# Attention and experts of eight images: the pairs of maxima in later images placed by another table

## The chip, the cores and the metric

The kernel runs on one core of a Trainium2 chip. The metric is the device time of one execution in microseconds, as the median of timed runs. The engines are TensorE (PE, its weight loads PEld), VectorE (DVE), ScalarE (ACT), GpSimd (POOL) and SyncE (SP), which here issues DMAs.

## The reference

One transformer layer with modulation (adaLN) over 8 images of 1024 tokens by 256 channels, in float32:

```python
mod = (silu(c) @ wmod)                 # sa, ca, ga, sb, cb, gb per image
h = layernorm(x) * (1 + ca) + sa
kv_c = rmsnorm(h @ W_kv) * g_kv;  q_c = h @ W_q
q, k = concat(content, rope(...))      # 16 heads of 16 + 32 channels
attn = softmax(causal(q @ k.T * scale))
x = x + ga * ((attn @ v) @ W_o)
h = layernorm(x) * (1 + cb) + sb
t = (h @ Wm + bm) in tokens x 8 heads of 32
w = softmax(t @ expert_emb); top 2 of 16 experts
out = sum over the 2: w * (gelu(t @ W1[e] + b1) @ W2[e] + b2)
x = x + gb * (out @ Wo + bo)
```

## The kernel before, in words

Each engine has its own program, and all five walk the same lists. An image has two parts. The attention part is 48 slots (`MAIN`): a slot is one group g of four heads, one half c of the queries (512 tokens) and one block j of 128 keys. `SEQ` orders the group-halves: slots 0 to 3 are (0,0), 4 to 7 (1,0), 8 to 15 (0,1), 16 to 19 (2,0), 20 to 23 (3,0), 24 to 31 (1,1), 32 to 39 (2,1), 40 to 47 (3,1). The last four blocks of each are diagonal and have 512, 384, 256 and 128 columns, the others 512. In a slot TensorE computes the scores in two steps of two heads (`scores(s, 0)`, `scores(s, 1)`, L1279), ScalarE takes the exponentials (L1393), and in even slots TensorE multiplies with the values of the two slots before (`values`, L1305). Four PSUM banks hold scores, two steps deep. The experts' part is 64 steps, with L1321, L1411, L1339, L1448 and L1518.

Softmax needs the maximum of each query's row before the scores are made. It enters as one more row of the queries, against minus ones in the keys. The maxima are computed apart, in "pairs": a pair is a tile of queries by keys for two heads (hh = 0, 1), two matmuls into two banks of a ring (L428), and two reads by VectorE, which take the maximum (L576; L573 where the causal mask is added, some of them in two pieces). Group g has five pairs for the first half (`PAIRS[0]`) and thirteen for the second (`PAIRS[1]`). When a group-half is done, an item `("row", g, c)` transposes the maxima (L500), VectorE copies them (L586), and SyncE sends them with four DMAs (L780) into the queries, on which the first scores of that group-half wait (semaphore `c_row..`). For the second half an `rmax` item (L582) joins two columns first.

`attend_slots(img)` writes the list of items by hand: each slot has three parts, "between" (after `scores(s, 0)`), "behind" (after `scores(s, 1)`) and "front" (after that), then come the values. Other items are `rope` (rotary parts, L477 or L479, L607, L608, and L726, L739 on GpSimd), `sums` (outputs divided, L505, L595, L598), `tr` (L510), `o` (output projection, L518, L634), `stats`, `xn`, `tr2`, `tm`, and `chain` (the router). All of them share one ring of three PSUM banks, in the order of the list; a pair takes two. `ring_write` waits for both banks before the pair's first matmul. An item's bank is free when its reader (VectorE, or ScalarE for some) has incremented `c_rd` or `c_ra`.

For images 1 to 7 `PLACES` gives each of the 47 pairs a slot and a part. Two pairs of group 1 were made in the experts' part of the image before (`AHEAD`). Image 0 has a list of its own, which the change leaves alone. In it, slot 12 holds three pairs (`(12, 3)` with part `2 * k // n`: two between, one behind), slot 22 holds one, and slot 25 holds two and a `sums` item.

VectorE also multiplies the gates into two projection weights and a bias, five instructions after the items of slot 22: `wog` (attention's projection), `wfg` (the last projection) and `bog`. TensorE waits for them once, before `("o", 0, 0)` in slot 32, and GpSimd before it adds `bog` at the start of the experts' part.

Of the kernel before, what the change touches and what calls it, by code (L numbers as in the profile page):

```python
# [23 lines left out]
CH = C // P  # L24
# [312 lines left out]
PAIRS = [masked_pairs(0), [(((i, 0, pr),),) for i in range(4, 8) for pr in range(2)]]  # L337
# [74 lines left out]
def item_matmuls(pe, L, R, item):  # L412
# [57 lines left out]
    elif kind == "rope":  # L470
        g, isk, c = rope_of(item[1], R.alone)
        if g < 2:
            R.wait(pe, L, ("ht", c, CH - 1) if isk else ("qct", c))
        hd = slice(g * HG * RD, (g + 1) * HG * RD)
        if isk:
            for k in range(CH):
                mm = pe.matmul(out, L.wkr[:, k, hd], L.ht[:, k, half(c)], start=(k == 0), stop=(k == CH - 1))  # L477
        else:
            mm = pe.matmul(out, L.wqr[:, hd], L.qct[:, half(c)], start=True, stop=True)  # L479
    elif kind == "sum":  # L480
        R.wait(pe, L, ("kvt",))
        for t in range(4):
            mm = pe.matmul(out[:, 2 * t:2 * t + 2], L.kvsq[:, t * P:(t + 1) * P], L.halves[:, :], start=True, stop=True)
    elif kind == "qc":
        h, c = item[1:]
        R.wait(pe, L, ("qct", c))
        mm = pe.matmul(out, L.wqc[:, h * P:(h + 1) * P], L.qct[:, half(c)], start=True, stop=True)  # L487
    elif kind == "std":
        pe.wait_ge(S["f_ks"], 1)
        for t in range(4):  # L490
            for c in range(2):
                mm = pe.matmul(out[KVR * c:KVR * c + KVR, t * P:(t + 1) * P],
                               L.kstd[:, 4 * c + t:4 * c + t + 1].broadcast_to([P, KVR]), L.ident[:, :], start=True, stop=True)
    elif kind == "row":
        g, c = item[1:]
        if c:
            pe.wait_ge(S["c_mf"] if g else S["f_mf"], max(g, 1))
        else:
            R.wait(pe, L, ("pair", g, *PAIRS[0][-1]))
        mm = pe.transpose(out[0:4 * HG, 0:P], L.mxf if c else L.mx0[:, g, :], L.ident[:, :])  # L500
    elif kind == "sums":
        m = item[1]
        pe.wait_ge(S["c_o"], m + 1)
        for t in range(4):
            mm = pe.transpose(out[:, t * P:(t + 1) * P], L.ot[:, m % 2, t * P:(t + 1) * P], L.ident[:, :])  # L505
    elif kind == "tr":
        c, j = item[1:]
        R.wait(pe, L, ("sums", SEQ.index((NG - 1, c))))
        for t in range(4):
            mm = pe.transpose(out[:, t * P:(t + 1) * P], L.ao[:, 4 * c + t, j * P:(j + 1) * P], L.ident[:, :])  # L510
    elif kind == "o":
        c, n = item[1:]
        R.wait(pe, L, ("tr", c, CH - 1))
        if c == 0:
            pe.wait_ge(S["d0_w"], 5)
        for t in range(2):
            for k in range(CH):
                mm = pe.matmul(out[:, t * C:(t + 1) * C], L.at[:, k, (2 * n + t) * P:(2 * n + t + 1) * P], L.wog[:, k, :],  # L518
                               start=(k == 0), stop=(k == CH - 1))
    elif kind == "tr2":  # L520
        c, j = item[1:]
        pe.wait_ge(S[f"d{c}_xn"], 4)
        for t in range(4):
            mm = pe.transpose(out[:, t * P:(t + 1) * P], L.xn2[:, t, j * P:(j + 1) * P], L.ident[:, :])
    elif kind == "tm":
        c, j = item[1:]
        R.wait(pe, L, ("tr2", c, CH - 1))
        for k in range(CH):
            mm = pe.matmul(out, L.wms[:, k, j * P:(j + 1) * P], L.h2t[:, k, :], start=(k == 0), stop=(k == CH - 1))  # L529
    elif kind == "lg":  # L530
        c = item[1]
        R.wait(pe, L, ("tm", c, CH - 1))
        for t in range(4):
            for j in range(CH):
                o = t * P + j * 4 * NE
                mm = pe.matmul(out[:, o:o + 4 * NE], L.t32[:, j, t * P:(t + 1) * P], L.embd[:, :], start=True, stop=True)  # L536
    elif kind == "gt":
        c = item[1]
        pe.wait_ge(S[f"d{c}_r"], 17)
        for t in range(4):  # L540
            mm = pe.transpose(out[:, t * P:(t + 1) * P], L.eb[:, t * FH:(t + 1) * FH, :].rearrange("p a b -> p (a b)"),
                              L.ident[:, :])
    elif kind == "out":
        n = item[1]
        pe.wait_ge(S["e_add"], 30 * (n // 2 + 1))
        for t in range(2):
            for k in range(CH):
                mm = pe.matmul(out[:, t * C:(t + 1) * C], L.ct[:, k, (2 * n + t) * P:(2 * n + t + 1) * P], L.wfg[:, k, :],  # L548
                               start=(k == 0), stop=(k == CH - 1))
# [553 lines left out]

AHEAD = 2
EARLY = 3
PLACES = [(1, 0), (2, 0), (3, 0), (5, 0), (7, 0)]
PLACES += [(s, part) for s in range(9, 37) for part in range(2 - s % 2)]


def attend_slots(img):  # L1110


    slots = [([], [], []) for _ in range(NM)]
    if img:
        slots[1][1].extend([("out", 2), ("out", 3)])
        places = PLACES
        pairs = [("pair", 1, *p) for p in PAIRS[1][AHEAD:AHEAD + 5]]
        pairs += [("pair", g, *p) for g in (2, 3) for p in PAIRS[0]]
        pairs += [("pair", 1, *p) for p in PAIRS[1][AHEAD + 5:]]
        pairs += [("pair", g, *p) for g in (2, 3) for p in PAIRS[1]]  # L1120
    else:
        per_slot = [(0, 2), (1, 2), (2, 3), (3, 2), (4, 3), (5, 3), (8, 2), (9, 1), (10, 2), (11, 2), (12, 3), (13, 1), (14, 2), (15, 1),
                    (16, 2), (17, 2), (18, 2), (19, 1), (20, 2)] + [(s, 1 if s in (22, 23, 27, 29, 31, 33) else 2) for s in range(21, 37)]
        places = [(s, 2 * k // n) for s, n in per_slot for k in range(n)]
        early, second = [("pair", 0, *p) for p in PAIRS[1][EARLY:]], [("pair", 1, *p) for p in PAIRS[1]]
        pairs = early[:1] + [("pair", 1, *p) for p in PAIRS[0]] + early[1:]
        pairs += second[:5] + [("pair", 2, *p) for p in PAIRS[0]] + second[5:6] + [("pair", 3, *p) for p in PAIRS[0]] + second[6:]
        pairs += [("pair", g, *p) for g in (2, 3) for p in PAIRS[1]]
        slots[2][1].append(("row", 1, 0))
        slots[6][0].append(("rmax", 0))  # L1130
        slots[6][1].append(("row", 0, 1))
    assert len(places) == len(pairs)
    ropes = {s: ("rope", 8 + k) for k, s in enumerate((0, 2, 3, 4, 5, 6, 7, 8) if img else (3, 5, 6, 7, 8, 9, 10, 11))}
    for (s, part), pair in zip(places, pairs):
        if part and img and s and s in ropes:
            slots[s][1].append(ropes.pop(s))
        slots[s][part].append(pair)
    for s, rope in ropes.items():
        slots[s][1].append(rope)
    for s, g in ((21, 1), (29, 2), (37, 3)):  # L1140
        slots[s][0].insert(0, ("rmax", g))
    for s, row in ((13, (2, 0)), (17, (3, 0)), (21, (1, 1)), (29, (2, 1)), (37, (3, 1))):
        slots[s][2].append(("row", *row))
    for m, gc in enumerate(SEQ[:-1]):
        last = max(s for s, step in enumerate(MAIN) if step[:2] == gc)
        slots[last + 2][2].append(("sums", m))
    slots[27][1].append(("tr", 0, 0))
    slots[28][1].append(("tr", 0, 1))
    slots[32][1].append(("o", 0, 0))
    slots[33][1].extend([("o", 0, 1), ("stats", 0)])  # L1150
    slots[34][1].append(("xn", 0))
    slots[37][1].extend([("tr2", 0, 0), ("tr2", 0, 1)])
    slots[38][1].append(("tm", 0, 0))
    slots[39][1].extend([("tm", 0, 1), ("tlo", 0, 0)])
    slots[40][1].extend([("tlo", 0, 1), ("lg", 0), ("chain", 0, 1), ("chain", 0, 2)])
    slots[41][1].append(("exp", 0))
    for k in range(3, 18):
        slots[41 + (k - 3) // 3][1].append(("chain", 0, k))
    slots[46][2].append(("gt", 0))
    return slots  # L1160
# [68 lines left out]
def all_images(nc, L, O):  # L1229
# [18 lines left out]
    with nc.Block() as block:  # L1248
# [182 lines left out]
        def _(v):  # L1431
# [29 lines left out]
            for img in range(B):  # L1461
                for s, (between, behind, front) in enumerate(aslots[img]):
# [6 lines left out]
                    if s == 22:  # L1469
# [3 lines left out]
                        for k in range(CH):  # L1473
                            v.tensor_tensor(L.wog[:, k, :], L.wos[:, k, :], L.gate[:, 0, :],
                                            ALU.mult).then_inc(S["d0_w"], 1)
                            v.tensor_tensor(L.wfg[:, k, :], L.wfs[:, k, :], L.gate[:, 1, :],
                                            ALU.mult).then_inc(S["d0_w"], 1)
                        v.tensor_tensor(L.bog[:, :], L.bor[:, :], L.gate[:, 1, :], ALU.mult).then_inc(S["d0_w"], 1)
# [214 lines left out]
```

## Time and profile before

| | us |
|---|---|
| median of 3 timed runs | 2917.65 (2917.25 to 2918.07) |
| the profiled execution | 2920.5 |
| its span, first to last instruction | 2918.1 |
| attention part of the third image (window) | 161.00 |

The span is what the trace shows; the profiled execution's own time has 2.4 us more around it. Busy time is an engine's union of instructions; a matmul's end is modelled, so a step of TensorE is best read as the distance between starts.

### The profile page before, as it was taken

The numbers are of one execution on the slowest core, as the hardware profiler recorded it, in microseconds if no ns is written. First come the engines' busy times: TensorE is split into PE (matmuls) and PEld (weight loads), VectorE is DVE, ScalarE is ACT, GpSimd is POOL, SyncE is SP. The second block draws the span as 40 slices with busy tenths as digits, with TensorE's granted clock in tenths as the row PEclk, the third lists the DMA queues.
The fourth block names the chain that finished last, engine by engine and source line by source line (L and its number), as shares of the span: only waits on it lengthen the run. The fifth ranks groups of instructions, "written<-read, shape, count | busy, mean of one in ns | idle before, by whom it ended". The sixth has DMA issues, their size and how long they took to land.

```text
span 2918.1 us, 50109 instructions
## 1 busy us (share of the span) xinstructions
PE 2816.6 (97%) x16476; PEld 1241.9 (43%) x16476; DVE 1863.0 (64%) x4638; ACT 1808.5 (62%) x2148; POOL 1246.2 (43%) x1325
## 2 busy tenths in 40 slices
PE   7899999999999999999999999999999999999999
PEld 3344444444444443444444444444444444444433
DVE  5775666756666666666667666675756657667553
ACT  2346675566755677457675576655666566665687
POOL 4312645136451364414654146531565215561254
PEclk9899999999999999999999999999999999999999
DMA  6203453044430444304432055311453124530343
GB/s 156 57 5 99 118 130 73 1 108 122 120 71 8 119 118 107 71 21 121 122 97 61 23 134 130 87 47 46 121 133 89 32 71 119 124 88 20 77 127 94
DMA packets 176972, 252.96 MB, mean 87 GB/s; under 512 B 50509, under 2 KB 83293, under 8 KB 176621
## 3 DMA queue, kind: packets, MB, share of 16 engines
q1 hardware_dynamic: 176100, 248.44, 34.3%
q8 instruction: 136, 2.23, 0.3%
q10 hardware_dynamic: 620, 1.34, 0.2%
q14 instruction: 116, 0.95, 0.1%
HBM read 159.13 MB, written 12.63 MB: 59 GB/s over the span
## 4 chain that ended last, share of the span: by engine, by line
PE 86%; DVE 7%; issue 3%; ACT 2%; POOL 1%; SPq 1%; DMA 1%; ACTq 0%; DVEq 0%; POOLq 0%
PE ps L1279 17%; PE ps L1321 17%; PE ps L1339 16%; PE ps L1305 9%; PE ps L428 7%; PE ps L477 4%; PE ps L479 2%; PE ps L518 2%; PE ps L548 2%; DVE rest L573 1%; PE ps L529 1%; PE ps L505 1%; PE ps L536 1%; PE ps L463 1%; PE ps L487 1%
## 5 line engine op out<-in xcount | busy, mean ns | idle before, releaser
L1411 ACT ACTIVATE rest<-ps 128x1024 f32<-128x1024 f32 x1024 | 993.8, 1024 | 341.1 <-PE ps L1321 340.9
L1393 ACT ACTIVATE rest<-ps 128x1024 f32<-128x1024 f32 (+3 forms) x768 | 610.2, 809 | 537.4 <-PE ps L1279 511.6
L1518 POOL TENSOR_TENSOR rest<-rest 128x512 f32<-128x512 f32 x478 | 632.0, 1322 | 560.7 <-DVE rest L1448 548.1
L1448 DVE SCALAR_TENSOR_TENSOR rest<-ps,b2c,wide 128x512 f32<-128x512 f32 x512 | 384.0, 750 | 489.8 <-PE ps L1339 451.7
L1321 PE MATMUL ps<-wide,w1s 98*128 98x512 f32 x2048 | 655.1, 437 | 11.5 <-ACT rest L1411 8.7
L1339 PE MATMUL ps<-rest,w2s 128*32 128x512 f32 x4096 | 546.1, 605 | 0.6 <-ACT rest L1411 0.6
L1508 POOL TENSOR_SCALAR_AFFINE_SELECT rest<-rest 128x256 f32<-128x256 f32 x512 | 206.4, 411 | 772.3 <-ACT rest L1393 770.3
L573 DVE CUSTOM_DVE_ANT_0 rest<-ps,maskd 128x512 f32<-128x512 f32 (+3 forms) x1024 | 444.8, 487 | 118.8 <-PE ps L428 114.0
L1279 PE MATMUL ps<-wide 49*128 49x512 f32 (+3 forms) x2304 | 486.3, 511 | 10.2 <-ACT rest L1393 4.2
L1321 PEld LDWEIGHTS ps<-wide,w1s 98*128 98x128 f32 x2048 | 340.8, 188 | 301.0 <-ACT rest L1411 189.0
L576 DVE TENSOR_REDUCE front<-ps 128x1 f32<-128x512 f32 x512 | 329.0, 684 | 92.9 <-PE ps L428 88.7
L428 PE MATMUL ps<-wide 48*128 48x512 f32 (+3 forms) x1152 | 269.9, 500 | 37.8 <-DVE front L573 20.7
L1305 PE MATMUL ps<-rest,front 128*32 128x512 f32 (+3 forms) x3072 | 290.2, 496 | 0.0
L1279 PEld LDWEIGHTS ps<-wide 49*128 49x128 f32 x2304 | 195.5, 186 | 195.7 <-issue 121.3
L726 POOL TENSOR_TENSOR front<-front,sin 128x512 f32<-128x512 f32 x128 | 163.7, 1279 | 110.5 <-DVE front L607 110.2
L428 PEld LDWEIGHTS ps<-wide 48*128 48x128 f32 x1152 | 108.0, 187 | 219.1 <-DVE front L573 79.1
L1279 PE MATMUL ps<-heads 49*128 49x512 f32 (+3 forms) x768 | 168.0, 520 | 2.8 <-DMA heads<-front 2.6
L739 POOL TENSOR_TENSOR front<-front 128x512 f32<-128x512 f32 x128 | 163.0, 1273 | 10.0
L1339 PEld LDWEIGHTS ps<-rest,w2s 128*32 128x32 f32 x4096 | 80.6, 108 | 191.0 <-issue 189.5
L1305 PEld LDWEIGHTS ps<-rest,front 128*32 128x32 f32 x3072 | 80.7, 110 | 163.0 <-issue 113.5
L477 PE MATMUL ps<-front,wkr 128*128 128x512 f32 x256 | 125.5, 619 | 0.0
L1279 PEld LDWEIGHTS ps<-heads 49*128 49x128 f32 x768 | 66.7, 191 | 66.0 <-issue 43.8
(142 smaller groups left out, 2192.4 us busy)
## 6 DMA issues: line engine op xcount, KB each, us to landing
wide<-gate_rows SPq DMA_DIRECT2D x1024, 128.0 KB, 2.8
wide<-front SPq DMA_DIRECT2D x480, 64.0 KB, 2.0
wide<-front SPq DMA_DIRECT2D x192, 128.0 KB, 2.3
ao<-in_x SPq DMA_DIRECT2D x16, 512.0 KB, 5.1
heads<-front SPq DMA_DIRECT2D x64, 128.0 KB, 2.3
xs<-in_x SPq DMA_DIRECT2D x16, 512.0 KB, 5.0
out<-xs SPq DMA_DIRECT2D x32, 256.0 KB, 2.7
wide<-ao SPq DMA_DIRECT2D x96, 64.0 KB, 2.3
```

What stands on the lines that cost most here:

```text
L428: mm = pe.matmul(outs[hh][:, at:at + w], L.q2[g][rows, pr, i * P:(i + 1) * P].bitcast(F32R), L.k2[g][rows, pr, keys].bitcast(F32R), start= ...
L477: mm = pe.matmul(out, L.wkr[:, k, hd], L.ht[:, k, half(c)], start=(k == 0), stop=(k == CH - 1))
L573: ins = v.tensor_tensor_reduce(out=R.junk[hh][:, at:at + w], in0=src[:, at:at + w], in1=L.maskd[:, HALF - w:], scale=1.0, scalar=-3e38, op ...
L576: ins = v.tensor_reduce(dst, src[:, 0:w], AX.X, ALU.max)
L1279: mm = pe.matmul(bank(2 * (u % 2) + hh)[:, 0:HALF - f], L.k2[g][rows, pr, j * P:(j + 1) * P], L.q2[g][rows, pr, c * HALF + f:(c + 1) * HAL ...
L1305: mm = pe.matmul(bank(PVB)[h * VW:(h + 1) * VW, f:HALF], L.va[:, j, HG * g + h, :], L.pt[:, u % PTS, h % 2, f:HALF], start=(j == 0), stop= ...
L1321: mm = pe.matmul(bank(2 * (u % 2) + k), L.w1s[:, e, :], L.x2[:, c, 4 * j + 2 * p + k, :], start=True, stop=True)
L1339: mm = pe.matmul(bank(L2 + q % 2)[FD * h:FD * h + FD, :], L.w2s[:, e, :], L.hm[:, (2 * q + h // 2) % HM, (h % 2) * HALF:(h % 2 + 1) * HALF ...
L1393: nc.scalar.activation(L.pt[:, u % PTS, :, f:HALF], L.ps[:, 2 * (u % 2):2 * (u % 2) + 2, 0:HALF - f], ACT.Exp, scale=SCALE).then_inc(S["c_ ...
L1411: nc.scalar.activation(L.hm[:, u % HM, :], bank(2 * (u % 2), 2), ACT.Gelu).then_inc(S["e_gelu"], 1)
L1448: v.scalar_tensor_tensor(out=dst, in0=bank(L2 + q % 2), scalar=L.b2c[:, e:e + 1], in1=L.gb[:, q // 2 % GB, q % 2, :], op0=ALU.add, op1=ALU ...
L1518: g.tensor_tensor(dst, dst, L.gy[:, k % GY, :], ALU.add).then_inc(S["e_add"], 1)
```

## The change

The 47 pairs of images 1 to 7 are given other slots. Group 1 now has seven early pairs (was five) before the first-half pairs of groups 2 and 3. Slots 4 and 8 each get a pair; slots 9 to 36 hold one each, but for the slots in `SHARE`, which hold 0, 2 or 3. The part of pair k of n in a slot is `2 * k // n`, so of three pairs two are between and one is behind, and of two one is between and one behind. The count of pairs by slot, before and after:

| slot | 4 | 8 | 14 | 16 | 18 | 20 | 22 | 24 | 25 | 26 | 27 | 28 | 29 | 30 | 32 | 33 | 34 | 35 | 36 |
|---|---|---|---|---|---|---|---|---|---|---|---|---|---|---|---|---|---|---|---|
| before | 0 | 0 | 2 | 2 | 2 | 2 | 2 | 2 | 1 | 2 | 1 | 2 | 1 | 2 | 2 | 1 | 2 | 1 | 2 |
| after | 1 | 1 | 1 | 1 | 1 | 1 | 1 | 0 | 2 | 3 | 2 | 3 | 2 | 1 | 1 | 2 | 1 | 2 | 3 |

The other slots keep their count. In all images the last projection's weight `wfg` and bias `bog` are formed after the items of slot 39 instead of slot 22, and TensorE waits for `d0_w` at 2 instead of 5 before slot 32's projection.

```diff
@@ item_matmuls, kind "o"
         if c == 0:
-            pe.wait_ge(S["d0_w"], 5)
+            pe.wait_ge(S["d0_w"], CH)
@@
-PLACES = [(1, 0), (2, 0), (3, 0), (5, 0), (7, 0)]
-PLACES += [(s, part) for s in range(9, 37) for part in range(2 - s % 2)]
+SOON = 7
+SHARE = {10: 2, 12: 2, 24: 0, 25: 2, 26: 3, 27: 2, 28: 3, 29: 2, 33: 2, 35: 2, 36: 3}
+PLACES = [(s, 0) for s in (1, 2, 3, 4, 5, 7, 8)]
+PLACES += [(s, 2 * k // SHARE.get(s, 1)) for s in range(9, 37) for k in range(SHARE.get(s, 1))]
@@ attend_slots
-        pairs = [("pair", 1, *p) for p in PAIRS[1][AHEAD:AHEAD + 5]]
+        pairs = [("pair", 1, *p) for p in PAIRS[1][AHEAD:AHEAD + SOON]]
         pairs += [("pair", g, *p) for g in (2, 3) for p in PAIRS[0]]
-        pairs += [("pair", 1, *p) for p in PAIRS[1][AHEAD + 5:]]
+        pairs += [("pair", 1, *p) for p in PAIRS[1][AHEAD + SOON:]]
@@ vector
                         for k in range(CH):
                             v.tensor_tensor(L.wog[:, k, :], L.wos[:, k, :], L.gate[:, 0, :],
                                             ALU.mult).then_inc(S["d0_w"], 1)
+                    if s == 39:
+                        for k in range(CH):
                             v.tensor_tensor(L.wfg[:, k, :], L.wfs[:, k, :], L.gate[:, 1, :],
                                             ALU.mult).then_inc(S["d0_w"], 1)
                         v.tensor_tensor(L.bog[:, :], L.bor[:, :], L.gate[:, 1, :], ALU.mult).then_inc(S["d0_w"], 1)
```

## Rows read from the trace of the kernel before

**Rows 1.** The page: the span, and TensorE's busy time.

```profile
span 2918.1 us, 50109 instructions
PE 2816.6 (97%) x16476; PEld 1241.9 (43%) x16476; DVE 1863.0 (64%) x4638; ACT 1808.5 (62%) x2148; POOL 1246.2 (43%) x1325
```

**Rows 2.** Window, third image's attention: stretch, length, busy PE PEld DVE ACT POOL, clock, DMA.

```profile
807.53:968.53 161.00, 156.08 (x1018) 70.71 (x1018) 104.60 (x299) 85.88 (x112) 48.63 (x82) 1.00 0.19 44
```

**Rows 3.** Windows, third image: slots 4, 14-15, 16-23, 24, 25, ..., 38-39.

```profile
823.78:828.40 4.62, 4.62 (x30) 1.78 (x29) 1.97 (x6) 1.94 (x2) 3.26 (x4) 1.00 0.28 70
...
859.08:864.50 5.42, 4.65 (x42) 2.24 (x41) 3.94 (x20) 2.36 (x5) 1.47 (x4) 1.00 0.01 2
...
864.50:886.48 21.98, 20.88 (x167) 10.75 (x167) 18.45 (x53) 12.45 (x19) 6.54 (x17) 1.00 0.01 3
886.48:890.60 4.12, 3.71 (x31) 1.50 (x31) 4.06 (x14) 2.36 (x3) 0.98 (x2) 1.00 0.00 0
890.60:893.34 2.74, 2.74 (x18) 1.30 (x14) 1.88 (x5) 2.08 (x3) 0.00 (x0) 1.00 0.00 0
893.34:897.87 4.53, 4.52 (x30) 1.52 (x29) 3.28 (x8) 2.60 (x3) 0.00 (x0) 1.00 0.00 0
897.87:900.61 2.74, 2.74 (x19) 1.30 (x15) 1.29 (x2) 1.49 (x2) 0.00 (x0) 1.00 0.00 0
900.61:905.79 5.18, 5.17 (x33) 1.94 (x33) 2.67 (x5) 3.67 (x5) 0.81 (x2) 1.00 0.01 3
905.79:913.03 7.24, 6.68 (x58) 3.36 (x54) 4.45 (x16) 3.21 (x6) 1.70 (x5) 1.00 0.01 1
913.03:922.96 9.93, 9.93 (x60) 5.96 (x61) 7.03 (x24) 5.05 (x6) 0.73 (x2) 1.00 0.01 2
922.96:930.63 7.67, 6.73 (x39) 2.39 (x38) 6.90 (x23) 3.07 (x3) 1.02 (x1) 1.00 0.00 0
930.63:935.14 4.51, 4.51 (x29) 1.44 (x29) 3.22 (x7) 3.07 (x3) 0.81 (x2) 1.00 0.00 0
...
937.76:945.09 7.33, 7.22 (x42) 2.99 (x41) 1.97 (x4) 3.05 (x6) 1.90 (x5) 1.00 0.09 20
```

**Rows 4.** Timeline of slot 18, third image: start, length, engine, line, idle before.

```profile
871.42 0.69 DVE L573 CUSTOM_DVE_ANT_0 rest<-ps,maskd 128x512 f32<-128x512 f32 x1
...
872.26 0.50 PE L428 MATMUL ps<-wide 48*128 48x512 f32 x2 [0.45 <-DVE front L573]
872.70 1.71 PE L1305 MATMUL ps<-rest,front 128*32 128x512 f32 x16
...
872.77 1.29 DVE L576 TENSOR_REDUCE front<-ps 128x1 f32<-128x512 f32 x2
```

**Rows 5.** Windows of the first image: slots 12, 22 and 25.

```profile
132.58:138.54 5.96, 5.01 (x33) 1.86 (x33) 5.33 (x19) 2.05 (x2) 3.32 (x4) 1.00 0.20 44
...
170.72:173.71 2.99, 2.99 (x30) 1.39 (x29) 2.76 (x13) 1.19 (x2) 0.81 (x2) 1.00 0.01 2
...
178.34:181.84 3.50, 3.31 (x22) 1.56 (x18) 2.68 (x11) 2.64 (x3) 0.00 (x0) 1.00 0.01 2
```

**Rows 6.** Timeline, first image: slot 12, then the row DMAs before slot 16.

```profile
134.90 0.49 PE L428 MATMUL ps<-wide 48*128 48x512 f32 x2 [0.95 <-DVE front L573]
135.21 1.04 PE L1279 MATMUL ps<-heads 49*128 49x512 f32 x4
...
144.89 2.51 SPq L780 DMA_DIRECT2D wide<-front  x4
...
148.50 1.22 PE L1279 MATMUL ps<-wide 49*128 49x512 f32 x2 [2.78 <-DMA wide<-front]
```

**Rows 7.** Timeline, third image: row DMAs of slots 13 and 29, last gate product.

```profile
860.01 2.54 SPq L780 DMA_DIRECT2D wide<-front  x4
...
886.57 0.63 DVE L1478 TENSOR_TENSOR rest<-bor,gate 128x256 f32<-128x256 f32 x1
...
908.47 2.42 SPq L780 DMA_DIRECT2D wide<-front  x4
```

## The prediction

> **What bounds the kernel now.** I read the page first. The span is 2918.1 us, and TensorE is busy for 2816.6 of them [rows 1]: it is the engine that the others have to keep fed, and time is won only by shortening its waits. The profiled execution took 2920.5 us, 2.4 around its span; the median of the timed runs is 2917.65. I add a difference in the span to that median.
>
> Then the windows. Images 1 to 7 run the changed list; the attention of the third image takes 161.00 us at a granted clock of 1.00 [rows 2]. I cut it at the first score matmul of each slot [rows 3] (slot 24 runs from 886.48, slot 28 from 900.61), and the other later images repeat these lengths. The clock is full in all of these windows, so it drops out of the sum.
>
> A pair is two matmuls on TensorE into two of the ring's three PSUM banks, and two reads by VectorE. The timeline of slot 18 [rows 4] has both costs. The first read of its first pair takes 0.69 us, two reads together 1.29. The second pair is released at 872.26, 0.15 after that read ends (871.42 + 0.69), with TensorE idle for 0.45 before it; 0.44 later the next work starts, so the pair's columns cost 0.43. Its own read starts 0.51 after it. So with three banks, pair B can't start until the first read of pair A is done: 0.51 + 0.69 + 0.15, some 1.35 after A's start, of which A itself covers 0.43. What lies between A and B covers more: scores have four records where a pair has two [rows 4, 6], two passes, so 0.86 for 512 columns and half of it for 256. Two pairs put side by side have nothing between them, and VectorE's 1.3 is then the pace.
>
> **The change, part by part.** It moves ten pairs and takes none away, so TensorE's own 0.43 each cancels over the sum; I keep it in each slot all the same. One pair each leaves slots 14, 16, 18, 20, 22, 30, 32, 34 and two leave 24; one each comes to 4, 8, 25, 26, 27, 28, 29, 33, 35, 36. Slots 26, 28 and 36 then hold three, by `2 * k // 3` two of them side by side between the scores.
>
> *Slots 4 and 8.* These slots are long (4.62, TensorE never idle, VectorE busy 1.97 [rows 3], slot 8 the same), so nothing but the pair's columns comes in: from below nothing, if they hide in the switches between score matmuls, which take the 0.57 that slot 4 has over its columns; from above 0.43. I take 0.29 each, nearer the columns. Together **+0.6**. POOL, busy 3.26 of the 4.62 with the rotary parts, gets more time and not more work.
>
> *Slots 14 and 15.* 5.42 now. Without the second pair and its wait TensorE would be done by 4.4. But the first scores of slot 16 need the row of maxima that slot 13 sends, and its four DMAs leave SyncE from 860.01 [rows 7]. Image 0 shows the price of that step: four such issues from 144.89, and scores that had waited for the DMA start at 148.50 [rows 6], 3.61 later. So slot 16 can't begin before 863.62, against 864.50 now. **-0.9**, where the wait for the bank and the 0.43 would have given -1.0.
>
> *Slots 16 to 23.* 21.98 now [rows 3]. Slots 16, 18, 20 and 22 come down to one pair. Image 0 already has slot 22, of the same shape, with one pair: 2.99 [rows 5]; I take it for all four (in slots 16 and 20 the scores are wider and the values behind them shorter, with the same columns in sum). The odd slots between keep what they hold, 7.3 together, so the stretch goes to 4 x 2.99 + 7.3 = 19.3: **-2.7**. The same from the other side: 21.98 less four pairs' columns (1.7) and two waits of 0.45 like that of [rows 4] (slots 18 and 22) gives -2.6. The rows of slots 17 and 21 still arrive some 0.3 us ahead of the scores that need them.
>
> *Slot 24.* 4.12 now; it is left without a pair. Its columns are then 2.35 us (scores 1.71, values 0.64), plus switches: slot 36 has 0.24 over its columns and slot 4 has 0.57 [rows 3]; with 0.36 it is 2.71. **-1.4**. VectorE's backlog, which made its two pairs wait, came from the five gate products after slot 22, the longest 0.63 [rows 7]. Three of the five move to slot 39; there VectorE is busy for 1.97 of 7.33 us [rows 3], so at most 3 x 0.63 = 1.9 us fit in its idle time: **0**. Were that cover gone, the router's chain behind them would start up to 1.9 us later; it has slots 41 to 46 before TensorE transposes what it makes. POOL and TensorE's wait for the gated weight (2 for 5) come long after either product: nothing.
>
> *Slot 25.* Image 0 has this slot with two pairs and the sums: 3.50 [rows 5], against 2.74. **+0.8**.
>
> *Slots 26, 28, 36: two pairs side by side.* Image 0's slot 12 is the same shape with the same three pairs, and takes 5.96 [rows 5], with TensorE idle for 0.95 before the second pair, behind VectorE [rows 6]. Slot 26 goes 4.53 to 5.96 and slot 36 4.51 to 5.96, **+2.9** together. Slot 28 has a transpose more; 5.18 + 0.43 + 0.96 = 6.57, **+1.4**. From below, the 0.43 of columns each and no wait; from above 1.1 of wait each, as slot 26 follows a loaded 25. I take image 0's.
>
> *Slot 27.* 2.74 now. Its two pairs have 0.86 of scores between them: the second waits 0.1, the transpose behind it 0.15 for a bank. 3.45: **+0.7**; from below 0.43.
>
> *Slots 29 to 31.* 7.24 now. Slot 29 has 384 columns: 0.64 between its two pairs, and the row's transpose behind waits for a bank too: 2.9 for the 1.93 that it has now, my estimate. Slot 30 loses pair and wait, which alone would give 3.0 and 1.07 for slot 31. But the row of maxima leaves SyncE at 908.47 now, 2.68 into slot 29 [rows 3, 7]; with a second pair read before it (1.29) and 0.2 of waiting for that pair's results, it leaves at 4.2. The scores of slot 32 may start 3.61 later, 7.8 after slot 29's start. TensorE would be there at 7.0, or 7.6 with the wait of slot 30's pair behind the copy. So 7.8: **+0.6**. Here the stall removed becomes another: what is late next is the row.
>
> *Slots 32 to 35.* 9.93 and 7.67 now. Slots 32 and 33 hold as many pairs as before, but 33 has two and the projection queued behind them for a bank: 10.3. Slot 34's second pair waits 0.9 now (TensorE is busy 6.7 of the 7.67), VectorE being full with statistics and sums; without it 4.1 for slot 34, and 2.7 for slot 35 with two pairs. +0.4 and -0.9: **-0.5**.
>
> Sum for an image: 0.6 - 0.9 - 2.7 - 1.4 + 0.8 + 2.9 + 1.4 + 0.7 + 0.6 - 0.5 = +1.5. Seven images: **+10 us**, 2917.65 + 10 = 2928. Put as waits: some 3.0 us go, some 4.5 come, because VectorE's 1.3 us a pair were spread over slots 14 to 24 and are now packed into 25 to 29 (twelve pairs in five slots, where seven were).
>
> A rule of the Trainium skill speaks for the edit. Perfetto Trace Analysis, section Matmuls, says that independent matmul groups should rotate through different banks, so that the evacuation of one overlaps the next group's matmuls. The ring rotates, yet image 0's slot 12 shows the wait all the same: rotation over three banks, two to a pair, doesn't cover two pairs in a row. By the rule alone the terms of slots 25 to 36 would shrink to columns, which is the first rival below.
>
> **The rivals.** *Faster: side by side costs only columns.* If VectorE catches up behind the scores, so that the waits in 26, 28 and 36 vanish (3 x 1.0), the sum is -1.5 an image, -10 us: 2907. If half of it vanishes, the image stands at 0. For it: in later images POOL and the DMAs are quiet in these slots. Against it: image 0's wait names VectorE's read, not those. It decides from the point where slot 26 or 36 takes under 5.3 us (4.5 + 0.43 + 0.3). The rule named above is this case.
>
> *No change: both halves even.* The waits for rows don't hold slots 16 and 32 (0.1 and 0.2 saved) and the doubled slots cost 0.7 each for 1.0 (0.9 saved): +0.3 an image, +2 us: 2920. For it: the row's arrival rests on one DMA wait of image 0. It holds if the first scores of slots 16 and 32 name no DMA.
>
> *Slower still: VectorE's backlog carries on.* If slots 27 and 29 wait for a full pair of reads too (1.3 each, of which I have 0.8 in the sum) it is 1.8 us an image more, 13 us: 2941. Against it: slot 30 and the row wait let VectorE catch up, and slots 38 and 39 leave it idle [rows 3].
>
> *The waits are not removed at all*: 2.7 an image back, 2947. Against it: slot 22 of image 0. No chance of its own.
>
> **How the numbers follow.** A measurement of this kernel tells 0.2%, 5.8 us, from no change. Forecast (+6 to +18 us) 0.50; slower still 0.10; even (within 5.8 either way) 0.21; faster 0.19. The forecast's own range is 2924 to 2936. Over all, leaving out most of the last and half of the faster case: 2911 to 2937. Faster 0.19, same 0.21, slower 0.60.
>
> **What would show it.** Slots 18, 22 and 34 near 3.0, 3.0 and 4.1 us; slot 24 near 2.7; slots 26 and 36 near 6.0 with TensorE idle before a pair behind VectorE; the first scores of slots 16 and 32 released by a DMA. The attention of an image goes from 161.0 to 162.5, the experts' part stays. Wrong it would be by the doubled slots above all: three terms of +1.4 that rest on one slot of image 0.

## The result, and the profile after

The changed kernel takes 2926.48 us (median of 5 runs, 2925.73 to 2934.74) against 2917.74 for the kernel before on the same chip: a ratio of 1.0034, 95% interval 1.0023 to 1.0045. Forecast was 2928, range 2911 to 2937, slower at 0.60. It is slower by 8.7 us.

Images are numbered from 0 (images 0 to 7), and "the third image" is image 2, "the eighth" image 7.

The profiled execution is the longest of the five: 2934.74 us, span 2933.0, which is 14.9 us over the profile before. Of these, 8.9 lie in the attention of images 1 to 7, 4.8 in that of image 0 and 1.6 behind the last attention. So its sum is not that of the median, and it is read by slots. The windows of the third image, cut at the first score matmul of each slot, answer to [rows 2, 3]; the columns are stretch, length, busy time of PE, PEld, DVE, ACT and POOL, granted clock, DMA share and GB/s:

```profile
812.15:973.54 161.39, 155.89 (x1019) 70.63 (x1018) 105.04 (x299) 85.77 (x112) 48.66 (x82) 1.00 0.19 44
828.40:833.26 4.86, 4.86 (x31) 1.98 (x31) 3.24 (x8) 2.05 (x2) 3.26 (x4) 1.00 0.31 79
864.21:868.77 4.56, 4.16 (x39) 2.00 (x38) 2.81 (x16) 2.50 (x5) 1.47 (x4) 1.00 0.01 2
868.77:887.92 19.15, 18.76 (x156) 9.65 (x156) 13.10 (x34) 12.23 (x19) 6.74 (x17) 1.00 0.01 3
887.92:890.63 2.71, 2.71 (x24) 1.11 (x25) 1.00 (x6) 1.68 (x3) 0.53 (x2) 1.00 0.00 0
890.63:893.95 3.32, 3.32 (x22) 1.63 (x18) 1.83 (x5) 2.93 (x4) 0.00 (x0) 1.00 0.00 0
893.95:900.09 6.14, 5.22 (x33) 1.72 (x32) 5.53 (x20) 2.05 (x2) 0.00 (x0) 1.00 0.00 0
900.09:903.44 3.35, 3.32 (x20) 1.52 (x17) 1.92 (x5) 2.05 (x2) 0.00 (x0) 1.00 0.00 0
903.44:909.97 6.53, 5.65 (x36) 2.12 (x35) 4.75 (x11) 3.22 (x4) 0.81 (x2) 1.00 0.01 3
909.97:917.55 7.58, 6.71 (x56) 3.26 (x52) 4.54 (x14) 3.27 (x6) 1.70 (x5) 1.00 0.01 1
917.55:927.57 10.02, 10.01 (x63) 6.05 (x63) 6.98 (x24) 4.99 (x6) 0.73 (x2) 1.00 0.01 2
927.57:934.13 6.56, 6.54 (x39) 2.50 (x40) 5.88 (x19) 3.35 (x4) 1.02 (x1) 1.00 0.00 0
934.13:940.14 6.01, 5.16 (x32) 1.62 (x28) 5.52 (x13) 2.79 (x3) 0.81 (x2) 1.00 0.00 0
```

Line by line against [rows 3], with what the prediction had:

| slots | before | after | difference | predicted |
|---|---|---|---|---|
| 4 (8 the same) | 4.62 | 4.86 | +0.5 for both | +0.6 |
| 14, 15 | 5.42 | 4.56 | -0.9 | -0.9 |
| 16 to 23 | 21.98 | 19.15 | -2.8 | -2.7 |
| 24 | 4.12 | 2.71 | -1.4 | -1.4 |
| 25 | 2.74 | 3.32 | +0.6 | +0.8 |
| 26 and 36 | 9.04 | 12.15 | +3.1 | +2.9 |
| 27 | 2.74 | 3.35 | +0.6 | +0.7 |
| 28 | 5.18 | 6.53 | +1.35 | +1.4 |
| 29 to 31 | 7.24 | 7.58 | +0.3 | +0.6 |
| 32 to 35 | 17.60 | 16.58 | -1.0 | -0.5 |
| whole attention | 161.00 | 161.39 | +0.4 | +1.5 |

Images 1, 3, 4, 5, 6 and 7 repeat these lengths but for drops of the clock and waits for rows of maxima, of which more below.

In the timeline of TensorE in slot 26 the two neighbours stand 1.34 us apart, and the second starts when VectorE has read the first's first bank (columns: start, length, engine, line, idle before and who ended it):

```profile
895.03 0.49 PE L428 MATMUL ps<-wide 48*128 48x512 f32 x2
896.37 0.51 PE L428 MATMUL ps<-wide 48*128 48x256 f32 x4 [0.85 <-DVE front L576]
```

Before slot 16 the scores now wait for the row of maxima, in the third image a little, in the eighth much. The row's DMAs and the scores of each, from the timelines:

```profile
865.14 2.53 SPq L780 DMA_DIRECT2D wide<-front  x4
...
868.77 1.13 PE L1281 MATMUL ps<-wide 49*128 49x512 f32 x4 [0.25 <-DMA wide<-front]
...
2648.32 2.54 SPq L780 DMA_DIRECT2D wide<-front  x4
...
2652.79 1.13 PE L1281 MATMUL ps<-wide 49*128 49x512 f32 x4 [1.09 <-DMA wide<-front]
```

868.77 - 865.14 = 3.63 is what [rows 6] gave (3.61). In the eighth image it is 4.47.

Before slot 32 the row's DMAs are on the chain too. `--critical` for the third image (start, length, what):

```profile
915.84 1.61 DMA wide<-front
917.45 0.10 issue
917.55 1.09 PE ps L1281 x3
```

The first issue was at 913.99, so slot 32 starts 3.56 after it. But slot 31 keeps the 1.07 us that it had before: the row arrives just when TensorE is ready, and costs nothing.

There is one thing more, which no slot of the third image shows. The seventh image's attention takes 163.23 us instead of 161.39. First the windows of that attention and of its slot 30, then TensorE's timeline there:

```profile
2237.67:2400.90 163.23, 157.49 (x1019) 70.84 (x1018) 105.01 (x299) 85.77 (x112) 48.65 (x82) 0.99 0.19 44
2338.42:2343.70 5.28, 4.76 (x29) 1.52 (x28) 2.72 (x11) 1.19 (x2) 1.21 (x3) 0.70 0.02 5
```

```profile
2339.64 0.56 PE L428 MATMUL ps<-wide 48*128 48x128 f32 x4 [0.52 <-DVE front L576]
2340.00 0.62 PE L1281 MATMUL ps<-wide 49*128 49x256 f32 x4
2340.56 3.22 PE L1307 MATMUL ps<-rest,front 128*32 128x512 f32 x16
```

Sixteen matmuls with the values take 3.22 us where they take 1.71 in [rows 4]: TensorE's clock has fallen from 2.4 to 1.2 GHz for 3.4 us (the granted clock of the window is 0.70), right behind the waits of slots 26, 28, 29 and 30. A drop makes its slot and the next 1.6 to 1.7 us longer (slots 30 and 31 here 6.47 for 4.85). This profile has three such drops between 160 and 2750 us, one in slot 26 of the fifth image and one in slot 30 of the seventh and eighth. The kernel before has none there.

### The profile page after: what moved, and what is told of

The parts are those of the page before. It is cut to its first block, busy times and chain, and to the rows that moved or that the text cites. A ratio compares the mean times of both kernels' runs of the same rounds, so it can differ in the third digit from the quotient of the medians.

```text
span 2933.0 us, 50109 instructions
## 1 busy us (share of the span) xinstructions
PE 2823.6 (96%) x16476; PEld 1243.5 (42%) x16476; DVE 1866.2 (64%) x4638; ACT 1807.8 (62%) x2148; POOL 1246.9 (43%) x1325
## 3 DMA queue, kind: packets, MB, share of 16 engines
q10 hardware_dynamic: 620, 1.34, 0.2%
## 4 chain that ended last, share of the span: by engine, by line
PE 85%; DVE 6%; issue 3%; SPq 2%; ACT 2%; DMA 2%; POOL 1%; ACTq 0%; DVEq 0%; POOLq 0%
PE ps L1281 18%; PE ps L1323 17%; PE ps L1341 16%; PE ps L1307 8%; PE ps L428 7%; PE ps L477 4%; PE ps L479 2%; PE ps L518 2%; PE ps L548 2%; DMA wide<-front 1%; PE ps L529 1%; PE ps L505 1%; PE ps L536 1%; SPq L780 1%; PE ps L463 1%
## 5 line engine op out<-in xcount | busy, mean ns | idle before, releaser
L1307 PE MATMUL ps<-rest,front 128*32 128x512 f32 (+3 forms) x3072 | 296.5, 505 | 0.0
```

Of the source, the lines that this page charges most:

```text
L1307: mm = pe.matmul(bank(PVB)[h * VW:(h + 1) * VW, f:HALF], L.va[:, j, HG * g + h, :], L.pt[:, u % PTS, h % 2, f:HALF], start=(j == 0), stop= ...
```

## The experiments

Each was timed together with the kernel before, whose medians were 2917.74, 2918.76, 2919.16 and 2918.64 us in the four groups of runs; a ratio is to that kernel on the same chip.

**Gates only.** The old table, with the second hunk of the change:

```diff
-            pe.wait_ge(S["d0_w"], 5)
+            pe.wait_ge(S["d0_w"], CH)
...
+                    if s == 39:
+                        for k in range(CH):
```

> Only the second part of the change: the last projection's weight and bias formed in slot 39, TensorE waiting for 2 of the gate products instead of 5, the table of pairs as before. Theory (VectorE's backlog behind the five products makes slot 24's pairs wait, 0.34 to 0.5 us an image): slot 24 goes from 4.12 to about 3.6 us, everything else stays; seven images, -3 to -4 us, about 2914. Rival (VectorE's time there is hidden, or the three products meet the router's chain in slots 40 to 45): no change or +2 us.

Measured: 2915.57 us, ratio 0.9988 (0.9979 to 0.9997). The window of slot 24, third image:

```profile
888.76:892.27 3.51, 3.44 (x30) 1.61 (x30) 3.12 (x12) 2.36 (x3) 0.73 (x2) 1.00 0.00 0
```

3.51 for 4.12, and the attention 160.41 for 161.00, in all seven images. The theory holds: VectorE's five products held up slot 24, and the three that move cost nothing in slot 39. This half of the change is a gain, of 3 us.

**Table only.** The new table, with all five products after slot 22:

```diff
-                    if s == 39:
-                        for k in range(CH):
```

> Only the first part of the change: the new table of pairs, all five gate products after slot 22. Theory (the table makes the whole change, since slot 24 has no pair that could wait for VectorE): the same as the changed kernel, 2926 within 3 us, and slots 26, 28 and 36 at 6.0 to 6.5 us. Rival (moving the products is what makes the table worse): back to 2918 or below.

Measured: 2928.09 us, ratio 1.0030 (1.0020 to 1.0040), slots 26, 28 and 36 at 6.14, 6.54 and 6.01 us. With the new table slot 24 holds no pair, so the gates' move has nothing left to give: the halves don't add. Two drops of the clock in images 1 to 7, one behind slot 26 and one behind slot 30.

**No two side by side.**

```diff
-SHARE = {10: 2, 12: 2, 24: 0, 25: 2, 26: 3, 27: 2, 28: 3, 29: 2, 33: 2, 35: 2, 36: 3}
+SHARE = {10: 2, 12: 2, 16: 2, 20: 2, 24: 0, 25: 2, 26: 2, 27: 2, 28: 2, 29: 2, 32: 2, 33: 2, 35: 2, 36: 2}
```

> The changed kernel, but the third pairs of slots 26, 28 and 36 moved to slots 16, 20 and 32, so that no two pairs stand side by side. Theory (two pairs side by side cost a wait of 0.85 us each, and with it now and then a drop of TensorE's clock): the three slots return to 4.6, 5.2 and 4.5 us, slots 16, 20, 32 take 0.45 more each, -2.9 us an image, -20 us against the changed kernel: 2906, and faster than the kernel before by 11. Rival (the price is VectorE's total load in slots 25 to 36, not the neighbours): the waits move to the slots that now hold two, and it stays within 5 us of the changed kernel's 2926.

Measured: 2907.60 us, ratio 0.9962 (0.9949 to 0.9974). Windows of slots 16, 26, 28, 32 and 36:

```profile
862.65:866.11 3.46, 3.44 (x28) 1.51 (x28) 2.89 (x10) 2.23 (x3) 1.27 (x4) 1.00 0.02 7
888.96:893.61 4.65, 4.65 (x30) 1.48 (x29) 4.07 (x14) 2.05 (x2) 0.00 (x0) 1.00 0.00 0
896.93:902.12 5.19, 5.18 (x34) 1.89 (x33) 3.49 (x9) 3.22 (x4) 0.81 (x2) 1.00 0.02 3
909.69:915.35 5.66, 5.49 (x39) 3.11 (x39) 4.39 (x13) 2.36 (x3) 0.74 (x2) 1.00 0.01 3
927.18:931.85 4.67, 4.67 (x30) 1.40 (x26) 4.21 (x10) 2.81 (x3) 0.81 (x2) 1.00 0.00 0
```

The three slots lose 1.5, 1.3 and 1.3 us; 16, 20 and 32 take 0.5, 0.5 and 0.7. Three pairs of 47 moved are 19 us, and they turn the sign. Slots 25 to 36 still hold 21 pairs of the 23, so VectorE's load there is nearly the same, and the waits of slots 29 and 30 stay (0.23 and 0.52) while only waits of 0.1 come in, in slots 32 and 33. So the 0.85 of slots 26, 28 and 36 is the neighbours' price, not the load's. No drops of the clock.

**A spread table.**

```diff
-SOON = 7
-SHARE = {10: 2, 12: 2, 24: 0, 25: 2, 26: 3, 27: 2, 28: 3, 29: 2, 33: 2, 35: 2, 36: 3}
-PLACES = [(s, 0) for s in (1, 2, 3, 4, 5, 7, 8)]
+SOON = 8
+SHARE = {10: 2, 12: 2, 16: 2, 20: 2, 24: 2, 26: 2, 27: 2, 28: 2, 32: 2, 35: 2, 36: 2}
+PLACES = [(s, 0) for s in range(1, 9)]
```

> A table worked out from the traces: a pair in each of slots 1 to 8, then two in slots 10, 12, 16, 20, 24, 26, 27, 28, 32, 35, 36 and one in the others; gates as in the changed kernel. Theory (second pairs cost only their columns in full-width slots, and waits of 0.45 to 0.9 us in slots of 256 columns; early slots take a pair for 0.24): against the kernel before -4.2 us an image, -29 us: 2888. Slots 14, 18, 22, 30, 34 at 3.0 to 4.0 us, slot 24 at 3.6. Rival (the row DMAs before slots 16, 24 and 32 take over): some 1 us of DMA wait an image at each, so 2905 or more.

Measured: 2899.95 us, ratio 0.9933 (0.9921 to 0.9946). Expected were 29 us off the kernel before, and 19 came. Part of the difference is slot 6, 4.69 us for 3.76:

```profile
832.79 0.51 PE L428 MATMUL ps<-wide 48*128 48x512 f32 x2 [0.42 <-DVE front L608]
```

The pair waits for VectorE's read of the rotary item before it (L608), as it does not in slots 4 and 8. The pair costs 0.93 there for the 0.24 expected: 4.8 us over seven images. The DMA wait before slot 16 (0.2 to 1.1) is here too, in images 4, 5 and 7 above all, and makes slot 15 longer by 2.7 us over the seven. The remaining 2 to 3 us were not traced.

**Rows sent earlier.**

```diff
-    for s, row in ((13, (2, 0)), (17, (3, 0)), (21, (1, 1)), (29, (2, 1)), (37, (3, 1))):
+    for s, row in ((12 if img else 13, (2, 0)), (16 if img else 17, (3, 0)), (21, (1, 1)), (29, (2, 1)), (37, (3, 1))):
```

> The changed kernel, with two rows of maxima of images 1 to 7 transposed, copied and sent a slot earlier: (2,0) after slot 12 and (3,0) after slot 16, where their last pairs are done. Theory (in the changed kernel the first scores of slot 16 wait for the row's DMAs, 0.1 to 1.0 us an image): the DMA wait before slot 16 is gone in all seven images, slot 15 at 1.07 us, 2 to 4 us less than the changed kernel, 2923; the waits in slots 26, 28 and 36 stay. Rival (the copy, earlier in VectorE's queue, delays a pair by as much): same as the changed kernel within 1 us.

Measured: 2927.44 us, ratio 1.0028 (1.0018 to 1.0037); the rival wins. Three drops of the clock in images 1 to 7 (two behind slot 30, one behind slot 36). The DMA wait is gone in all images (slot 15 at 1.07), but slot 16 is 0.87 longer than in the changed kernel and slot 17 0.2 shorter, and slots 12 to 14 (the other row) give and take 0.3: the row's transpose must wait until VectorE has read the pair just before it, and TensorE waits with it.

```profile
865.47 0.27 PE L500 MATMUL ps<-ident,front 128*16 128x128 f32 x1 [0.59 <-DVE front L573]
```

**Shorter reads.**

```diff
-                    ins = v.tensor_reduce(dst, src[:, 0:w], AX.X, ALU.max)
+                    ins = v.tensor_reduce(dst, src[:, 0:w // 2 if g > 1 else w], AX.X, ALU.max)
```

> The changed kernel, but VectorE reads only the first half of the columns of every unmasked pair of groups 2 and 3 (256 of 512; the maxima of the other half are left out). TensorE's work is the same. Theory (a pair next to another waits for the first read of its neighbour): in slot 26, where the first of the two is unmasked, the wait falls from 0.84 to 0.57 us, by the 0.27 that a read of 256 columns is shorter; in slots 28 and 36, where the first is masked and still read in full, it stays at 0.85 to 0.87. Slot 30's wait (0.52), which comes from VectorE's backlog behind slot 29, goes almost wholly. Rival (the wait is for the third bank's turn or TensorE's own switch, not for the read): 0.84 stays in slot 26.

Measured: 2900.89 us, ratio 0.9938 (0.9924 to 0.9952). TensorE in slot 26 of the third image:

```profile
885.51 0.51 PE L428 MATMUL ps<-wide 48*128 48x256 f32 x4 [0.58 <-DVE front L576]
```

0.58 for 0.84, as the theory had it to 0.01; in slots 28 and 36, whose first pair is masked and read in full, the waits stay at 0.88 and 0.85, and slot 30's falls under 0.2. So the wait is the neighbour's first read. No drops of the clock.

That one wait is 1.9 us over seven images, and by the medians the kernel is 25.6 us faster than the changed one. The rest, of which the expectation names only slot 30, is in slots 21, 25, 28, 29, 30, 33 and 36, each 0.15 to 0.5 us shorter (slot 36 takes 5.51 for 6.01, its 0.85 unchanged), and in the missing drops. So VectorE's load has a price of its own in slots 25 to 36, beside the neighbours' 0.85. The likely reason is that shorter reads free the pairs' banks sooner; no run took this apart.

**A better table.** Slot 6's pair goes to slot 11, and both rows are sent a slot earlier (the hunk above).

```diff
-SHARE = {10: 2, 12: 2, 24: 0, 25: 2, 26: 3, 27: 2, 28: 3, 29: 2, 33: 2, 35: 2, 36: 3}
+SHARE = {10: 2, 11: 2, 12: 2, 16: 2, 20: 2, 24: 2, 26: 2, 27: 2, 28: 2, 32: 2, 35: 2, 36: 2}
```

> The table worked out from the traces, mended by them: no pair in slot 6 (it cost 0.93 us there), two in slot 11 instead, and rows (2,0) and (3,0) sent a slot earlier. Theory: slot 6 gives back 0.93, slot 11 takes 0.3 (as slot 35, of the same shape, takes for its second pair), the DMA wait before slot 16 (0.1 to 1.0) goes: -1.0 us an image against the spread table's 2900, 2893. Rival (three slots in a row with two pairs, 10 to 12, bring the backlog back): waits behind VectorE of 0.4 or more in slot 12 or 14, and 2900 as before.

Measured: 2895.07 us, ratio 0.9915 (0.9902 to 0.9929). The attention of images 1 to 7 is 0.8 us shorter each than with the spread table, where 1.0 was expected; no pair of slots 12 and 14 waits 0.1 us or more in the third image, so the rival isn't seen.

**The changed kernel again.**

> The changed kernel once more, for a second profile. Theory (the waits of slots 26, 28 and 30 leave TensorE idle often enough that its clock falls now and then): one to three drops to half clock between 160 and 2750 us, right behind the wait of slot 26 or 30, where the kernels without side-by-side pairs and the kernel before show none; each costs 1.2 to 1.7 us. Rival (the drops of the first profile were chance): none.

Measured: 2933.11 us in one run, and four drops in images 1 to 7. They cost 1.6 to 1.7 us each. One is behind the wait of slot 26, one behind slot 30, and two behind slot 36, which neither this expectation nor the next one names.

**Filled waits.** In images 1 to 7, TensorE writes the first head's tile once more into the free bank, before it waits for the second:

```diff
+        if (g, *parts[0]) in FILL and R.filler:
+            out, at = ring_write(pe, L, R, item, 0), 0
+            for i, n, pr in parts:
...
+                pe.matmul(out[:, at:at + w], L.q2[g][0:QD, pr, i * P:(i + 1) * P].bitcast(F32R),
+                          L.k2[g][0:QD, pr, keys].bitcast(F32R), start=True, stop=True)
+                at += w
         outs = [ring_write(pe, L, R, item, hh) for hh in range(2)]
```

> The changed kernel, with TensorE kept at work in its new waits: the pairs of slots 26, 28, 29, 30 and 36 that wait for a bank first write their first head's tile once more than needed into the bank that is already free (0.43 us of columns each; the regular matmuls write the same values over it), then wait and go on. Nothing is left out. In five profiles with the new table's waits TensorE's clock fell to half two to four times in images 1 to 7, right behind slots 26 or 30; in the other kernels never. Theory (it is the idle time in those waits that brings it): the waits shrink by 0.43 each, the slots keep their lengths within 0.2 us, the drops are gone or at most one, and the median falls by 3 to 6 us, to 2921 to 2924. Rival (the drops come from something else, or the filler's columns cost time because the waits aren't long enough): two to four drops stay, or the slots grow, 2927 or more.

Measured: 2923.33 us, ratio 1.0019 (1.0010 to 1.0028). The expectation miscounts: profiles with the new table's waits and drops were four, not five, and three of their twelve drops lie behind slot 36. The filler and the pair in slot 26 of the third image:

```profile
895.14 0.50 PE L429 MATMUL ps<-wide 48*128 48x256 f32 x2
895.94 0.50 PE L439 MATMUL ps<-wide 48*128 48x256 f32 x4 [0.30 <-DVE front L587]
```

Idle 0.30 for 0.85, and the slot is as long as in the changed kernel (6.13). The other waits shrink by 0.2 to 0.5: slot 28 to 0.65, slot 36 to 0.34, slots 29 and 30 to under 0.15. The windows of the seventh image, attention and slot 30:

```profile
2235.94:2397.97 162.03, 157.72 (x1026) 71.66 (x1025) 105.07 (x299) 85.85 (x112) 48.78 (x82) 1.00 0.19 44
2337.13:2340.91 3.78, 3.64 (x31) 1.62 (x30) 2.73 (x11) 1.20 (x2) 1.21 (x3) 1.00 0.02 6
```

3.78 at a clock of 1.00, where the changed kernel's profile has 5.28 at 0.70. No drop in images 1 to 7, against 3, 4, 2 and 3 in the changed kernel, its repeat, the table alone and the early rows. In those four profiles twelve of 28 images have a drop; were the filler without effect, seven images in a row without one would have a chance of some 0.02 ((16/28) to the seventh, if images are independent). So the filler's effect on the clock is well supported by one profile, not proven. That more work for TensorE made the kernel faster rests on this: the medians differ by 4 us against their own kernel before, and their intervals overlap (1.0010 to 1.0028 and 1.0023 to 1.0045).

**Only one row earlier.** The better table, with row (3,0) back after slot 17:

```diff
+    for s, row in ((12 if img else 13, (2, 0)), (17, (3, 0)), (21, (1, 1)), (29, (2, 1)), (37, (3, 1))):
```

> The mended spread table with only row (2,0) sent a slot earlier and row (3,0) back after slot 17, since sending it after slot 16 made TensorE wait 0.6 us for its pair there. Theory: slots 16 and 17 together 0.05 to 0.2 us shorter than with both rows early, no DMA wait before slot 16, now and then 0.1 before slot 20: 0 to -1 us against 2895, not to be told apart. Rival (slot 20's row becomes late by as much as slot 16's was): +0.1 to +0.5 us an image, 2896 to 2898.

Measured: 2893.08 us, ratio 0.9917 (0.9903 to 0.9930), not to be told from the 0.9915 of both rows. The attention of the third image:

```profile
802.87:960.18 157.31, 155.39 (x1019) 70.88 (x1018) 104.80 (x299) 86.12 (x112) 48.65 (x82) 1.00 0.19 45
```

161.00 before, so 3.7 us an image. Both versions beat both kernels by 24 us or more.

## Why the prediction was right, and where it was not

*The path of a pair.* Right. The interval of 1.35 us for two pairs in a row was measured at 1.34, and the shortened read moved it by just its own 0.27. Image 0's slot 12 was a true sample for slots 26, 28 and 36: 12.15 us for two of them where 11.92 was said.

*The waits removed.* Right, slot by slot: 18 and 22 at 2.9, 34 at 4.0, 24 at 2.71. The stall before slot 16 became a DMA wait, as said; 3.61 us from first issue to scores held in images 1 to 3. In images 4 to 7 it was 4.0 to 4.5, and slots 14 and 15 gave back up to all of their 0.9. The rows of slots 17 and 21, said to arrive 0.3 us ahead of their scores, did so in most images. In the third, slot 24's scores waited 0.27 for the DMAs, and slots 16 to 23 took 19.15 where images 1, 4 and 5 have 18.9.

*Slots 29 to 31.* Right in mechanism, 0.2 too dear. The row's first DMA left 4.02 us after slot 29's start, where 4.2 was said, and slot 32's scores came 3.56 after it, released by the DMA: 7.58 for 7.8. The pair of slot 30 waited 0.52 for VectorE's backlog, the second candidate (7.6), and TensorE came at the same moment. Where a drop of the clock had made slot 30 longer, the row was long in place.

*The sum of an image.* The step "Sum for an image: ... = +1.5" was too high. Measured without clock drops it is, in the filled kernel's images 1 to 7, 1131.2 us against 1127.0 before: +0.6 an image, +4.2 in all. The changed kernel's own profile agrees: 1135.9, less three drops of 1.6 to 1.7, is 1131. The mis-sized terms are slots 32 to 35 (-1.0 for -0.5), 29 to 31 (+0.3 for +0.6) and 25 (+0.6 for +0.8); the others are off by 0.2 or less and nearly cancel. The two largest misses were put together by hand from waits. Slot 25 was read from image 0, like slots 26 and 36, and like them is within 0.2.

*The clock.* The step that failed is "The clock is full in all of these windows, so it drops out of the sum". It was full in the kernel before. With the new waits it falls two to four times in seven images, at 1.6 to 1.7 us each, 3 to 7 us in all. 4.2 and three drops make 9.1, near the 8.7 measured (how many drops the unprofiled runs had isn't known), and 4.2 alone is near the filled kernel's 4.7 (2923.33 - 2918.64). So that the total came within 1.3 us of the forecast's 10 is partly luck, through two errors of opposite sign: waits too dear by 6 us, the clock left out at some 5.

*The gates.* Right at nothing, beside the new table; beside the old one they are worth 3 us, which the prediction, having emptied slot 24 first, did not ask.

*The rule of the Trainium skill* (Perfetto Trace Analysis, section Matmuls). The banks rotate and the wait is there. The shortened read shows what limits it: with three banks and two to a pair, the second of a pair's two reads is hidden behind the next pair, but the first only if other matmuls lie between them.

*The rivals.* Faster, if neighbours cost only columns: refuted by the slots of 6.0 to 6.5 us. Even: the first scores of slots 16 and 32 do name a DMA. Slower still, by the backlog: slots 27 and 29 took 3.35 and 2.73 us, not more than the forecast's 3.45 and 2.9.

*The late rows.* In images 4, 5 and 7 the row for slot 16 lands late in the kernel before too, 4.0 to 4.2 us after its first issue; there the scores came at 4.49 and hid it. What the late ones have in common stands in the DMA view. Here are the queues in the changed kernel, from the row's first issue to slot 16's scores, in the eighth image (late) and in the third (on time); columns are queue and kind, packets, MB, share of the 16 engines:

```profile
q8 instruction: 1, 0.02, 1.5%
q1 hardware_dynamic: 32, 0.01, 0.9%
q14 instruction: 1, 0.01, 0.4%
...
q1 hardware_dynamic: 32, 0.01, 1.1%
```

The twelve traces hold 384 rows sent before slots 16, 20, 24 and 32. In 68 of them an 8 KB packet of queue q14 (kind "instruction") starts 2.3 to 3.3 us after the row's first issue, and these rows land 3.61 to 4.44 us after it. The 316 others, packets of q8 or earlier and later ones of q14 included, land at 3.46 to 3.61. That is a coincidence without exception, but no run moved such a packet on purpose, and how it delays the row isn't shown.

*What stays open.* Why the clock falls in some images and not in others with the same waits. With the shortened reads the waits of 0.88 and 0.85 in slots 28 and 36 stayed, and it fell in none of seven images. And the first image's attention is 193 to 200 us long in different profiles, by stretches of half clock, though no table changes its pairs; this makes single profiles differ by about as much as the change.

## What to carry to other kernels

Count what lies between two users of a small ring before how many fall into a stretch: three pairs out of 47, placed beside a neighbour, decided the sign. A slot of the same kernel that already holds the new arrangement, here in the first image, prices it to 0.2 us, where sums of waits missed by up to 0.5. And where new waits are added to an engine whose clock can fall, a full clock in the old profile is no evidence for the new one: leave room for it. Keeping the engine at work through the wait is worth a trial: it held the clock up in the one profile taken.

## What the runs showed of the hardware that was not expected

- Behind waits of 0.84, 0.87, 0.22 and 0.52 us within 18 us (slots 26 to 30) TensorE's clock fell to 1.2 GHz for 3.4 us in six of 28 images, behind the first of these waits in three more, and behind the 0.85 of slot 36 in three; in the other images, with the same waits, it did not. A wait of 0.92 us in slot 34 of the kernel before never came with a drop in its seven images. With a 0.43 us matmul of no use inside these waits the clock stayed up in seven images of seven.
- Four row DMAs of the same size, issued over the same 2.5 us (2.8 in image 4), let their reader go 3.6 us after the first issue in images 1 to 3 and 4.0 to 4.5 us after it in images 4 to 7. In the twelve traces the 68 rows with an 8 KB packet of queue q14, kind "instruction", starting 2.3 to 3.3 us after their first issue land up to 0.8 us later than the latest of the other 316.
- A pair added in slots 4 and 8 cost 0.24 us, though its columns are 0.43. The prediction's reason, that part hides in the switches between score matmuls, was not tested.
